# A fused four-layer kernel: the fourth attention taken in two halves of the batches, with its value-times-output folds made one batch at a time in two column halves

## The reference

```python
def _L3_xattn_ref(hidden_states, cross_attention_states, attention_mask, ...):
    # 32 heads of 128, 8 key/value heads (groups of 4 heads), 64 keys per batch
    q = rmsnorm(q_proj(hidden_states), q_norm_w)      # per head
    k = rmsnorm(k_proj(cross_attention_states), k_norm_w)
    v = v_proj(cross_attention_states)
    scores = einsum('bhqd,bhkd->bhqk', q, k) * scale + attention_mask
    attn = softmax(scores)
    out = einsum('bhqk,bhkd->bhqd', attn, v).transpose(0, 2, 1, 3).reshape(B, Q, 32 * 128)
    return out @ o_proj_w.T
x = x + tanh(g_xattn[3]) * _L3_xattn_ref(layernorm(x), ctx, ...)
x = x + tanh(g_ffn[3]) * _L3_ffn_ref(layernorm(x), ...)      # with 50 Sinkhorn steps
```

## Time and profile before

| | us |
|---|---|
| median of 3 runs | 1476.28 (1474.4 to 1477.14) |
| profiled execution, its own time | 1476.89 |
| its span | 1475.2 |
| PE busy | 1320.4 (90%) |
| DVE busy | 1131.6 (77%) |
| ACT busy | 731.1 (50%) |
| POOL busy | 368.3 (25%) |

### The profile page before, as it was taken

One profiled execution on the slowest core, in us unless ns is written; L12 is line 12 of the kernel. 1 busy time (PEld: TensorE's weight loads), 2 busy tenths in 40 slices (PEclk: granted clock), 3 DMA queues, 4 the chain that ended last, 5 costly groups with the idle time before them and its releaser, 6 DMA issues.

```text
span 1475.2 us, 18889 instructions
## 1 busy us (share of the span) xinstructions
PE 1320.4 (90%) x6460; PEld 986.1 (67%) x6460; DVE 1131.6 (77%) x2109; ACT 731.1 (50%) x1549; POOL 368.3 (25%) x418
## 2 busy tenths in 40 slices
PE   7999999999998989978999998999999999998105
PEld 5665566556577758647888876777777777777102
DVE  4788988898887776876555577777677677778998
ACT  4777777787623754432222235555464555554004
POOL 1112212121146461233111022121321212212620
PEclk9999999999998999979999998999999999999557
DMA  6678977797830011243211310210201201000001
GB/s 223 165 174 186 248 210 167 195 246 195 201 109 1 2 58 42 47 92 80 72 46 56 110 43 1 72 57 16 72 6 66 72 0 72 0 1 1 0 0 57
DMA packets 37912, 127.76 MB, mean 87 GB/s; under 512 B 4944, under 2 KB 10960, under 8 KB 31680
## 3 DMA queue, kind: packets, MB, share of 16 engines
q1 hardware_dynamic: 26304, 83.38, 16.2%
q0 software_dynamic: 11520, 43.26, 15.5%
HBM read 72.63 MB, written 10.75 MB: 57 GB/s over the span
## 4 chain that ended last, share of the span: by engine, by line
PE 54%; DVE 23%; ACT 7%; DVEq 5%; issue 4%; DMA 4%; POOL 1%; POOLq 1%; SPq 0%
PE PS L150 11%; PE PS L152 11%; PE PS L151 11%; DVE AR L676 4%; PE PS L939 4%; PE PS L976 3%; DMA AR<-AR 3%; ACT s_sb L606 2%; DVE AR L2749 2%; DVE AR L2738 2%; DVE AR L2745 2%; DVE AR L682 2%; DVEq L666 2%; PE PS L962 1%; PE PS L535 1%
## 5 line engine op out<-in xcount | busy, mean ns | idle before, releaser
L438 POOL DMA_DIRECT2D AR<-AR x76 | 73.3, 1080 | 330.2 <-DVE AR L695 133.2
L1242 DVE TENSOR_TENSOR R16r<-PS,R16r 64x512 fp32r<-64x512 f32 x128 | 88.1, 688 | 56.4 <-ACT R16r L1097 55.4
L151 PE MATMUL PS<-R16r 128*128 128x512 f32 (+1 forms) x328 | 123.0, 375 | 0.0
L510 PE MATMUL PS<-R,HT 128*128 128x256 f32 x512 | 116.5, 381 | 3.6 <-ACT R L595 3.6
L152 PE MATMUL PS<-R16r 128*128 128x512 f32 (+1 forms) x312 | 119.1, 382 | 0.0
L535 PE MATMUL PS<-R,PT 128*128 128x512 f32 x256 | 116.1, 596 | 3.3 <-DVE X L716 3.3
L510 PEld LDWEIGHTS PS<-R,HT 128*128 128x128 f32 x512 | 94.7, 190 | 16.7 <-ACT R L595 5.0
L606 ACT ACTIVATE s_sb<-PS,sm 128x64 f32<-128x64 f32 x256 | 78.2, 338 | 52.5 <-DVE sm L701 51.8
L1097 ACT CAST R16r<-PS 64x512 fp32r<-64x512 f32 x128 | 74.4, 581 | 49.8 <-PE PS L939 48.9
L1102 ACT COPY AR<-PS 128x512 f32<-128x512 f32 x64 | 37.5, 586 | 123.9 <-PE PS L152 123.9
L150 PE MATMUL PS<-HTr,R16r 128*128 128x512 f32 (+1 forms) x240 | 91.0, 379 | 4.2 <-DVE R16r L190 2.7
(11 more groups left out here) (329 smaller groups left out, 3579.5 us busy)
## 6 DMA issues: line engine op xcount, KB each, us to landing
AR<-AR POOLq DMA_DIRECT2D x76, 528.0 KB, 6.5
OR<-in_wo SPq DMA_DIRECT2D x12, 1024.0 KB, 12.7
dequantised<-AR SPq DMA_DIRECT2D x8, 1056.0 KB, 5.8
WR<-in_w0q SPq DMA_DIRECT2D x8, 1024.0 KB, 11.5
AR<-in_w3q SPq DMA_DIRECT2D x8, 1024.0 KB, 6.6
WR<-dequantised SPq DMA_DIRECT2D x22, 256.0 KB, 2.8
AR<-in_nf SPq DMA_DIRECT2D x4, 1056.0 KB, 9.3
nf_in<-in_nf SPq DMA_DIRECT2D x4, 1056.0 KB, 12.4
```

What stands on the lines that cost most here:

```text
L151: nc.tensor.matmul(out, ah, bl, start=False, stop=False)
L438: nc.gpsimd.dma_start(nf_below(g)[:, part], what[:, part], accum_op=ALU.add, max_dma_last_dim=4 * N_NF // 2).then_inc(added, 16)
L510: i = nc.tensor.matmul(bank(2 + u % 2)[:, tt * 256:(tt + 1) * 256], HT0[:, c, tok], m[:, :, c * B + b, :], start=c == 0, stop=c == C - 1)
L1242: i = nc.vector.tensor_tensor(VOl[rows, h // 2, b, :], bank(7)[rows], VOh[rows, h // 2, b, :].bitcast(F32), ALU.subtract)
```

## The change

The units are reordered: all eight groups for batches 0 and 1, and then all eight again for batches 2 and 3 (`G, o = divmod(u, 2)`, 16 half-groups `NHG`). The keys and values of batches 2 and 3 are made with those of batches 0 and 1 and kept in `OT` (`KEPT`). The query and output weights are loaded, and the query weights split, once per half-group: 16 times where it was 8. A fold is now made for one batch and two heads as two matmuls that write the two halves of the bank, so ACT and DVE take it in one instruction of 128 partitions, and no swap is needed. The folds of unit u + 1 are made in unit u. The layer norm's tiles 4 to 7 move from ahead of the loop into units 0 to 3, through bank 7. All turns of the last layer norm stand in the last unit.

```diff
-        VOh = R16r[:, 4096:8192].rearrange("p (r b n) -> p r b n", r=2, b=B)
-        VOl = R16r[:, 8192:12288].rearrange("p (r b n) -> p r b n", r=2, b=B)
+        VOh = R16r[:, 4096:6144].rearrange("p (s r n) -> p s r n", s=2, r=2)
+        VOl = R16r[:, 6144:8192].rearrange("p (s r n) -> p s r n", s=2, r=2)
+        KEPT = OT[:].rearrange("p (g w n) -> p g w n", g=NG, w=2)
+        NHG = 2 * NG
...
+        def batch3(u):
+
+            return 2 * (u // 16) + u % 2
+
+        PIECE_ORDER = [("kv", 0), ("k", 0), ("f", 0, 0), ("f", 0, 1), ("kv", 1)]
+        for u in range(NU0):
+            PIECE_ORDER += [("n6", 4 + u)] if u < 4 else []
+            PIECE_ORDER += [("f", u + 1, 0)] if u + 1 < NU0 else []
+            PIECE_ORDER += [("k", u // 2 + 1)] if u % 2 == 0 and u // 2 + 1 < NG else []
+            PIECE_ORDER += [("f", u + 1, 1)] if u + 1 < NU0 else []
+            PIECE_ORDER += [("kv", u // 2 + 2)] if u % 2 and u // 2 + 2 < NG else []
...
-                v = SWAPPED if h % 2 else kvs[:, 256:256 + B * SK]
-                nc.tensor.matmul(o, v[:, 2 * bp * SK:2 * (bp + 1) * SK], wo3(g)[:, h * D:(h + 1) * D],
-                                 start=True, stop=True).then_inc(A3["piece_mm"], 1)
+                for hh in range(2):
+                    h = 2 * pr + hh
+                    i = nc.tensor.matmul(o[SK * hh:SK * (hh + 1), :], v_turned(G)[:, u % 2 * SK:(u % 2 + 1) * SK],
+                                         wo3(G)[:, h * D:(h + 1) * D], start=True, stop=True)
+                i.then_inc(A3["piece_mm"], 1)
...
+            fold_outputs(0, 0)
             queries(0, 0)
...
-            fold_outputs(0, 0, 0)
+            fold_outputs(0, 1)
             turn_q(0, 1)
             queries(1, 0)
-            fold_outputs(0, 0, 1)
             queries(1, 1)
-            pe_norm_tile(pe, 6, 4)
-            pe_norm_tile(pe, 6, 5)
             scores(0)
             turn_q(1, 0)
-            fold_outputs(0, 0, 2)
-            pe_norm_tile(pe, 6, 6)
-            pe_norm_tile(pe, 6, 7)
+            keys_values(1)
             turn_q(1, 1)
-            fold_outputs(0, 0, 3)
             scores(1)
...
+                if u < 4:
+                    late_norm(u + 4)
                 if more:
                     queries(u + 2, 1)
                     turn_q(u + 2, 0)
-                for f in folds(u, 1):
-                    fold_outputs(*f)
+                if u + 1 < NU0:
+                    fold_outputs(u + 1, 0)
                 outputs(u, 0)
...
                 outputs(u, 1)
-                for f in folds(u, 2):
-                    fold_outputs(*f)
+                if u + 1 < NU0:
+                    fold_outputs(u + 1, 1)
                 if more:
                     scores(u + 2)
-                if b == 1 and g + 1 < NG:
-                    keys_values(g + 1)
+                if o and G + 2 < NG:
+                    keys_values(G + 2)
...
-                for rows, b in fold_halves(bp, h):
-                    i = nc.scalar.copy(VOh[rows, h // 2, b, :], bank(7)[rows])
...
+                nc.scalar.copy(VOh[:, u % 2, pr, :], bank(7)).then_inc(A3["piece_hi"], 1)
...
-                for rows, b in fold_halves(bp, h):
-                    i = nc.vector.tensor_tensor(VOl[rows, h // 2, b, :], bank(7)[rows], VOh[rows, h // 2, b, :].bitcast(F32),
-                                                ALU.subtract)
-                i.then_inc(A3["piece_lo"], 1)
...
+                nc.vector.tensor_tensor(VOl[:, u % 2, pr, :], bank(7), VOh[:, u % 2, pr, :].bitcast(F32), ALU.subtract)\
+                    .then_inc(A3["piece_lo"], 1)
```

More of the change, by code:

```diff
@@ L167, in norm_bank @@
                 return bank(3)
+            if n == 6 and t >= 4:
+                return bank(7)
             return bank(t % 4 if n == 7 else NORM_BANKS[n][t % 2])
@@ L831, in fold_halves, with wo3 @@
-        def fold_halves(bp, h):
-            first, second = (2 * bp, 2 * bp + 1) if h % 2 == 0 else (2 * bp + 1, 2 * bp)
-            return ((slice(0, SK), first), (slice(SK, 2 * SK), second))
-        def sp_x3(sp):
[L837 to L850, removed]
+        def wo3(G):
+            return OR[:] if G % 2 == 0 else WR[:, 0:HG * D]
@@ L919, in keys_values @@
                     at = c * 2 * DH + DH
-                    i = nc.tensor.matmul(o[:, 256:512], WKV3[:, at:at + DH], CT[:, c, :], start=c == 0, stop=c == C - 1)
+                    i = nc.tensor.matmul(o[:, 256:512], w[:, at:at + DH], CT[:, c, :], start=c == 0, stop=c == C - 1)
                 i.then_inc(A3["piece_mm"], 1)
             def turn_k(g):
-                o = piece(PIECES3 * g + K_AT) if g else bank(2)
+                o = piece("k", g) if g else bank(2)
                 pe.wait_ge(A3["kn_ready"], g + 1)
@@ L1098, in folded_high @@
+            def keys(g):
+                act.wait_ge(A3["piece_mm"], made3("k", g))
+                for G in (g, g + NG):
+                    at = G // NG * 2 * SK
+                    i = nc.scalar.activation(k_turned(G), bank(7 if g else 2)[:, at:at + 2 * SK], ACT.Copy,
+                                             scale=qkw[:, 0:1])
                 i.then_inc(A3["piece_hi"], 1)
+            def folded_high(u, pr):
+                act.wait_ge(A3["piece_mm"], made3("f", u, pr))
+                nc.scalar.copy(VOh[:, u % 2, pr, :], bank(7)).then_inc(A3["piece_hi"], 1)
@@ L1167, in act_x3 @@
                     query_turned(u + 2, 0)
-                for f in folds(u, 1):
-                    folded_high(*f)
+                if u + 1 < NU0:
+                    folded_high(u + 1, 0)
                 if more:
@@ L1172, in act_x3 @@
                     query_turned(u + 2, 1)
-                if b == 2 and g + 1 < NG:
-                    keys(g + 1)
-                if b < 2 and g + 1 < NG:
-                    high_q(g + 1, (2 * b, 2 * b + 1))
-                for f in folds(u, 2):
-                    folded_high(*f)
-                if b == 1 and g + 1 < NG:
-                    keys_values(g + 1)
-            act_norm(act, 7, (3, 4, 5))
+                if o == 0 and G + 1 < NG:
+                    keys(G + 1)
+                if G + 2 < NHG:
+                    high_q(G + 2, (2 * o, 2 * o + 1))
+                if u + 1 < NU0:
+                    folded_high(u + 1, 1)
+                if o and G + 2 < NG:
+                    keys_values(G + 2)
+            act_norm(act, 7, range(T - 2))
             nc.scalar.preload_act_table_set("natural_log_exp_and_others")
@@ L1303, in dve_x3 @@
                 probs_low(u)
-                if b == 2 and g + 1 < NG:
-                    key_squares(g + 1)
-                for f in folds(u, 0):
-                    folded_low(*f)
+                if u < 4:
+                    low((u + 4,))
+                if u < 3:
+                    scaled((u + 5,))
+                if o == 0 and G + 1 < NG:
+                    key_squares(G + 1)
                 if more:
@@ L1326, in dve_x3 @@
                 add(u, 1)
-                for f in folds(u, 2):
-                    folded_low(*f)
-                if g == NG - 1 and b < B - 1:
-                    dve_stats(dve, b)
+                if u + 1 < NU0:
+                    folded_low(u + 1, 1)
+                if u in (NU0 // 2, NU0 // 2 + 2):
+                    dve_stats(dve, (u - NU0 // 2) // 2)
+                if u == NU0 - 2:
+                    dve_stats(dve, 2)
             dve.drain()
```

296 lines of the change are left out of this document (149 added, 147 removed).

## The result

The changed kernel takes 1487.93 us (median of 4 runs, 1486.78 to 1488.08), the kernel before 1476.71 us (4 runs beside them, 1474.4 to 1478.34). The ratio is 1.0075, with a 95% interval of 1.0058 to 1.0093: slower, by 11.2 us. Forecast were 1482.5 us and a range of 1474 to 1490. The profiled execution has a span of 1486.2 us and an own time of 1488.08.

The account below looks back on a forecast made before the run. PE bounds the kernel, busy 343.15 of 350 us in the steady part. 18.6 - 7.9 - 1.1 - 3.5 = +6.1 us on 1476.9 gives 1483.0, or 1482.5 us as a median; range 1474 to 1490.

Parts of the forecast that it names:

- The signs that were named: Profile after: plain unit 13.8 us, no idle ahead of keys and values, PE idle nearly 0, fold groups at 64 instructions.
- The folds: On PE in the loop: 60 excursions into column halves at 0.31 us each, +18.6 us, bounds 15.0 and 21.6.
- Half of the way out: Return from halves to full width, bounded by 0 and 0.11 us a fold; half was taken.
- The rival of a cheap switch: Switching costs only 0.1 us a fold beside fp32r products and scores: 1469.8 us; chance 0.13.
- serial halves: Rival: a fold's two halves run one after the other, 0.86 us more a fold, 1535 us; chance 0.02.
- Keys, values and `turn_k`: PE's waits in the loop go: seven of 1.13 us ahead of keys and values, -7.9; turn_k's, -1.1 us.
- The cover of 0.2 us that I called thin: Ahead of keys and values, scores covers 1.7 us, the fold's low part needs 1.5; failure returns part of the wait.
- Ahead of the loop: Start-up up to the first turn_p: -3.5 us, bounds -5 and 0, with queries starting 5.1 us later.
- the rival that the start gives nothing: No gain ahead of the loop, because PE's half clock comes anyway: 1486 us; chance 0.10.
- The end: From the last scores to the end of unit 31: 0, unit 31 ending within 1.5 us of before.
- At no cost: Query weights' second splitting on ACT and POOL and 16 MB more weight loads in the loop hold up nothing.

Follow-up runs that it names:

- b_keys: Kernel before with the next group's keys_values one step later on PE, behind the next unit's first queries, its ACT copies behind the probabilities': 1467.78 us, ratio 0.9953.

## Why the prediction was right, and which term failed

The direction, the mechanism and the order of magnitude held; the time was 5.4 us too low. The signs that were named came: 13.8 us for a plain unit, no idle time ahead of keys and values, PE busy throughout the steady part, the two fold groups at 64 instructions and half the time. That the time stayed within the range owes something to errors of opposite sign, as the terms show.

- **The folds**, forecast +18.6 (60 x 0.31): the full price is paid behind fp32r products and `scores` too. Excursion by excursion the trace has 0.35, which makes +20.8; three ways to get at it agree (0.69 a unit in the changed kernel, 0.67 to 0.69 with the halves alone, 19.6 to 20.7 us against full-width folds). Half of the way out, which I took because no row showed those neighbours, was the wrong half: the 0.36 of the earlier trace rows was the better estimate. A term mis-sized by 2.2 us. The rival of a cheap switch is out, and so is that of serial halves: two halves take 1.00 us alone and 0.94 in pairs, never 1.7.
- **Keys, values and `turn_k`**, forecast -9.0 for seven: all of these waits went, and the six groups there cost 1.49 less each, where I had 1.29. Right; at seven groups it would be -10.4. The cover of 0.2 us that I called thin never failed. The moves without halves (`b_keys`) win 7.8, which agrees.
- **Ahead of the loop**, forecast -3.5: this is the step that failed. Measured from the end of the stage before, `turn_p(0)` came 0.4 us later than it had, not 3.2 earlier, and with keys done ahead, four tiles' turns left over and a new `turn_k` wait in unit 0 (1.5 us of idle time, 1.8 with the restart) the sum is about +0.6 instead of -3.5. Three things were missing from my list. The first fold stands before the queries and PE is idle for 2.5 us ahead of it, and PE is granted half clock right behind that, from 876.1 to 879.5 us, which I had named as possible; counted in the same way from the keys' last matmuls in the stage before, the first queries start 6.6 us later than in before (24.0 instead of 17.4), where I had 5.1. POOL's scaling and split for the second unit stand before its norm pairs, and hold up DVE's scaling for 6.3 us with the first probabilities queued behind it; I had listed PE's and DVE's streams, not POOL's. And `turn_k` in unit 0 waits for a fold's low part by 1.5 us, since DVE is late there. The first two are tested, in the traces only: moving POOL's pairs takes the wait of 1.6 us away, moving the folds back brings `turn_p` 4.6 us forward; `turn_k`'s I only read in the trace. So the rival that the start gives nothing, which I gave 0.10 and 1486 us, is what happened there.
- **The end**, forecast 0: +1.0, within my 1.5. Beyond it the last logits end 2.6 us later. That stretch is in the windows above, at granted clock 0.55 though PE was busy throughout: the last 24 records took 5.16 us. In the kernel with POOL's pairs moved the same 24 took 2.76, so it is not a lasting effect of the change; why the clock falls there stays open.
- **At no cost**: right in the loop, where PE waits neither for the second splitting nor for the doubled traffic.

Adding up against my sum: 2.2 (folds) - 1.4 (keys) + 4.1 (start) + 1.0 (end), and -0.7 for what lies outside the change's steps (-2.3 in the stages before, +2.6 at the last logits, -1.0 in the rest), makes +5.2 on +6.1, so 11.3 where 11.2 lie between the two profiled executions. Those outside are not claimed as effects of the change: no run ties them to it.

## What to carry to other kernels

Column halves run side by side at the price of one full matmul, but each trip out of full width and back costs 0.35 us of TensorE: count the trips, not the matmuls, and put all narrow work of a unit into one (two trips a unit, one, none: 1488, 1477, 1467 us here, the last with half of the products left out). Work taken off an engine is worth only what the bound engine waited for it, and such a wait can often be had for nothing by moving one step (7.8 us here). A start-up sequence needs the list of every engine and queue in it, POOL's too, since a wait there has three queues behind it.

## What the runs showed of the hardware

- The price of a change of width does not depend on the neighbours that were tried: 0.10 us in behind fp32 transposes and 0.09 behind fp32r products, 0.14 to 0.15 within the stretch of halves, and about 0.10 out into either fp32r products or 64-column scores. I had expected fp32r neighbours to hide part of it.
- PE's granted clock fell to half (the 1.2 GHz level) behind an idle time of 2.5 us at 876.1 for 3.4 us, and again at the last logits with no idle time right ahead, where a record of 24 columns took 0.215 us instead of 0.115. It also fell behind 2.25 us of idle time at 1350 (0.55 over the next 3.5 us), as in the kernel before behind 2.72 us at 1344 (0.53 over 3.5). The same idle time in the kernel with POOL's pairs moved brought 6.8 us of it; without the idle time (first folds moved back) there was none at the start.
